# Four-layer stage of a language-model tower: layer norms as eight 64-column operations with two per-partition scalars, in place of two operations of 512 columns

## The reference, cut to what matters

```python
def _layernorm(x, g, b):
    mu = x.mean(-1, keepdims=True)
    var = ((x - mu) ** 2).mean(-1, keepdims=True)
    return (x - mu) * jax.lax.rsqrt(var + EPS) * g + b

for i in range(4):
    h = _layernorm(x, ln1_g[i], ln1_b[i])
    x = x + _linear_attn(h, Wq[i], Wk[i], Wv[i], Wo[i], bo[i])
    h = _layernorm(x, ln2_g[i], ln2_b[i])
    x = x + (gelu(h @ W1[i] + b1[i]) @ W2[i] + b2[i])
```

## Time and profile before

| what | before |
|---|---|
| device time, median of 3 runs (lowest to highest) | 598.67 us (596.02 to 600.78) |
| span of the profiled execution | 593.9 us |
| PE / DVE / ACT busy over the span | 90% / 70% / 64% |
| DVE instructions | 1114 |
| four-layer stage (first second-layer norm to the norm behind the last beat) | 254.2 to 443.5 us of the span |
| mean granted TensorE clock | 0.971 |

### The profile page before, as it was taken

The page is one execution under the profiler, slowest core; times in us unless marked ns, Lnnn a source line. Parts: engine busy times, 40 slices in busy tenths (PEclk is TensorE's granted clock), DMA queues, the critical chain, the costliest instruction groups (busy, mean ns, idle before and its releaser), DMA issues.

```text
span 593.9 us, 8251 instructions
## 1 busy us (share of the span) xinstructions
PE 534.8 (90%) x2798; PEld 279.4 (47%) x2798; DVE 413.9 (70%) x1114; ACT 381.5 (64%) x619; POOL 16.9 (3%) x29
## 2 busy tenths in 40 slices
PE   1898899999999997779999999999847999999995
PEld 1555685334333333656666676666524333333331
DVE  6887797566627555898999999999876336334343
ACT  0379746655666653448888887888734656765653
POOL 4060000000000000000000000000000000000000
PEclk9989998999999998979999999999988999999998
DMA  7910010422131313000000000000000312222220
GB/s 202 252 26 1 6 49 1 128 53 72 37 93 43 95 59 106 1 1 1 1 1 1 1 2 1 1 1 1 1 1 4 108 54 72 76 81 81 69 89 18
DMA packets 26840, 28.08 MB, mean 47 GB/s; under 512 B 12240, under 2 KB 17392, under 8 KB 26736
## 3 DMA queue, kind: packets, MB, share of 16 engines
q1 hardware_dynamic: 24496, 26.98, 16.1%
q10 hardware_dynamic: 2304, 0.58, 0.6%
HBM read 26.24 MB, written 1.31 MB: 46 GB/s over the span
## 4 chain that ended last, share of the span: by engine, by line
PE 51%; DVE 32%; issue 6%; ACT 6%; DMA 3%; SPq 1%; DVEq 0%; ACTq 0%
PE bank L1509 21%; PE bank L1520 20%; DVE l1mom L1240 3%; DVE Xs L1233 3%; DMA Ph<-in_itok 2%; PE bank L1355 2%; DVE Xn L1265 2%; DVE small L1201 2%; DVE Cen L1246 2%; DVE Mm L1226 1%; DVE ksm L1170 1%; DVE Ph L1195 1%; DVE small L1189 1%; ACT Hd L735 1%; PE bank L1422 1%
## 5 line engine op out<-in xcount | busy, mean ns | idle before, releaser
L647 ACT ACTIVATE Hd<-bank,b1all 128x512 f32<-128x512 f32 x256 | 154.9, 688 | 89.0 <-PE bank L1509 88.9
L1520 PE MATMUL bank<-Hd,w2m 128*64 128x512 f32 x512 | 123.7, 605 | 0.9 <-DVE Rest L1084 0.9
L1084 DVE SCALAR_TENSOR_TENSOR Tmp<-bank,b2col,Wb 128x512 f32<-128x512 f32 x56 | 42.0, 750 | 105.7 <-PE bank L1520 104.8
L1520 PEld LDWEIGHTS bank<-Hd,w2m 128*64 128x64 f32 x512 | 31.2, 136 | 85.9 <-issue 80.3
L1509 PE MATMUL bank<-Ph,w1m 64*128 64x512 f32 x256 | 65.2, 628 | 1.3 <-DVE Sc L1015 1.3
L1509 PE MATMUL bank<-XT,w1m 64*128 64x512 f32 x256 | 65.3, 625 | 0.0
L735 ACT ACTIVATE Hd<-bank,lvecs 128x512 f32<-128x512 f32 x64 | 38.7, 688 | 3.3 <-PE bank L1678 3.1
L1509 PEld LDWEIGHTS bank<-XT,w1m 64*128 64x128 f32 x256 | 23.0, 190 | 37.5 <-issue 18.9
L1629 PE MATMUL bank<-bd,XT 128*128 128x128 f32 x256 | 35.9, 285 | 5.2 <-ACT Hd L735 5.1
L1629 PEld LDWEIGHTS bank<-bd,XT 128*128 128x128 f32 x256 | 32.0, 196 | 17.8 <-ACT Hd L735 16.8
L1088 DVE TENSOR_TENSOR Rest<-Rest,Tmp 128x512 f32<-128x512 f32 x56 | 38.7, 692 | 1.9
(11 more groups left out here) (212 smaller groups left out, 825.6 us busy)
## 6 DMA issues: line engine op xcount, KB each, us to landing
Wb<-gate_rows SPq DMA_DIRECT2D x128, 128.0 KB, 2.9
Ph<-in_x SPq DMA_DIRECT2D x4, 512.0 KB, 9.3
Ph<-in_itok SPq DMA_DIRECT2D x4, 384.0 KB, 10.0
w1m<-in_w1e SPq DMA_DIRECT2D x1, 1028.0 KB, 19.2
w2m<-in_w2e SPq DMA_DIRECT2D x2, 512.0 KB, 13.7
w1m<-in_w1e SPq DMA_DIRECT2D x1, 1024.0 KB, 5.5
out<-Hs SPq DMA_DIRECT2D x16, 64.0 KB, 2.1
Hd<-in_w1all SPq DMA_DIRECT2D x1, 512.0 KB, 15.0
```

Of the source, the lines that this page charges most:

```text
L647: ac.activation(Hd[:, st.ring, k // 2, k % 2, :], bank[k][:, :], func, bias=b1all[:, st.m, st.e, k // 2:k // 2 + 1]).then_inc(up_read, 1)
L1084: ve.scalar_tensor_tensor(dst, bank[st.down_bank][:, :], b2, Wb[:, st.t % RING, :], ALU.add, ALU.mult).then_inc(down_read, 1)
L1520: ins = te.matmul(bank[st.down_bank][h * D:(h + 1) * D, :], w2m[:, st.e, hc * D:(hc + 1) * D], Hd[:, st.ring, hc, h, :], start=(hc == 0), ...
```

## The change

The helper centre and its semaphores go. scaled now makes a whole norm from Xs: for each of the eight tiles of a group one tensor_scalar instruction on 64 columns subtracts the tile's mean and multiplies with its inverse root, both read as per-partition scalars (128x1 each). Every one of the eight raises normed by one, so the counts that the matrix engine waits for are multiplied with E = 8; first_norms, which feeds the same semaphore before the beats, raises it by 8 at once.

```diff
-        centred = [sem(f"centred{w}") for w in range(2)]
@@ first_norms
-                                     ALU.mult).then_inc(normed[0], 1)
+                                     ALU.mult).then_inc(normed[0], E)
@@ 
-            def centre(job, w, ring, nth):
-
-                dve.wait_ge(l1_means[w], 4 * nth)
-                ve.tensor_tensor(tiles(Cen, job.g), tiles(Xs, job.g), wide(l1mom[:, ring, w, :, 1], E),
-                                 ALU.subtract).then_inc(centred[w], 1)
@@ 
-            def scaled(job, w, nth):
+            def scaled(job, w, ring):
 
                 rstep.settle()
-                dve.wait_ge(centred[w], nth)
-                ve.tensor_tensor(tiles(Xn, job.g), tiles(Cen, job.g), wide(l1stat[:, 2, w * E:(w + 1) * E], E),
-                                 ALU.mult).then_inc(normed[w], 1)
+                x, y = tiles(Xs, job.g), tiles(Xn, job.g)
+                for e in range(E):
+                    ve.tensor_scalar(y[:, e, :], x[:, e, :], l1mom[:, ring, w, e, 1:2],
+                                     l1stat[:, 2, w * E + e:w * E + e + 1], ALU.subtract,
+                                     ALU.mult).then_inc(normed[w], 1)
@@ beat of VectorE
-                if old:
-                    centre(old, 0, old.ring, old.done)
                 if now:
                     queries_shift(now)
@@ 
                     roots(attn, old)
-                    centre(attn, 1, attn.ring, attn.done)
                 if old:
-                    scaled(old, 0, old.done)
+                    scaled(old, 0, old.ring)
                 if attn:
-                    scaled(attn, 1, attn.done)
+                    scaled(attn, 1, attn.ring)
@@ beat of the matrix engine
-                    pe.wait_ge(normed[0], now.done)
+                    pe.wait_ge(normed[0], E * now.done)
@@ 
-                    pe.wait_ge(normed[1], feed.done)
+                    pe.wait_ge(normed[1], E * feed.done)
```

## The result

The changed kernel takes 615.68 us (median of 4 runs, 613.21 to 619.2) against 597.35 of the kernel before (4 runs, 595.54 to 600.78): a ratio of 1.030, 95% interval 1.025 to 1.035. The forecast was 614.5 us, in a range of 601 to 623. The profiled span grew from 593.9 to 614.2 us.

The account below looks back on a forecast made before the run. DVE's own instruction order was taken to bound beats 3 to 14; +15.0 us from twelve two-norm beats and +0.84 from beats 1 and 16, in all +15.8 on the 598.7 us median, gave 614.5 us, range 601 to 623.

Parts of the forecast that it names:

- DVE's order bounds beats 3 to 14: Four-layer stage: DVE's own instruction order sets the 12.04 us beat, so each us added there moves the end as much.
- The step: Start-to-start time of each new 64-column tensor_scalar with two per-partition scalars: 0.229 us, both scalars paid in full.
- the rival of the free scalars: Rival for the new instruction: scalars cost nothing in a row, step 0.098 us, kernel faster at 592.6 us; chance 0.07.
- the second scalar that comes with the first: Rival for the new instruction: the second scalar adds nothing, step 0.165 us, total 601.3 us; chance 0.12.
- one column at a time: Rival: the short instruction runs at single rate, step 0.263 us, total 621.7 us; 0.11, shared with otherwise dearer steps.
- At no cost: In a beat, the earlier shift, the residual add and their banks, 0.60 us earlier, were to add nothing.
- the prediction's own sign of being wrong: Wrong if the step is below 0.15 us, or a beat grows by other than sixteen steps less 2.41 us.
- the sum: Total added time: +15.0 us from twelve beats with both norms, +0.84 from beats 1 and 16, in all +15.8.
- Beats 2 and 15 hide their norm: One-norm beats ending in DVE waits for ScalarE of 1.48 and 1.47 us, which were to hide the +0.42 us.
- Beats 1 and 16: One-norm beats with the norm on the path: +0.42 us each, 1.83 for 1.41, together +0.84.
- The gain that a cheaper step could bring: In a beat of the stage, at most 0.40 us before DVE waits for ScalarE's exponential.
- The granted clock stays 1.00: The matrix engine was to keep its full clock from 282 us on; losing it, 638 us, had chance 0.04.

Follow-up runs that it names:

- half tiles: The changed kernel with every 64-column operation cut into two of 32 columns and the counts of normed doubled: one run of 666.67 us.
- the kernel with constants: The changed kernel with two constants in place of the two per-partition scalars, mean and inverse root left out of both norms: 597.67 us, 0.998 of the kernel before.

## Why the prediction was right, point by point

- **DVE's order bounds beats 3 to 14, and a loss there is paid in full.** Right: no wait of DVE for another engine in the changed kernel, a beat of 13.38 us for 13.3 foretold.
- **The step.** Right: 0.223 for 0.229 us, 308 ns for "about 0.31". The experiments with no and one scalar give 0.10 and 0.163, where the bounds taken from the earlier trace rows were 0.098 and 0.165. So the rival of the free scalars and that of the second scalar that comes with the first both fall, and the half tiles exclude one column at a time, by which 32 columns less would have taken 33 ns off the step and not 16.
- **At no cost.** Here a step failed. I said that the earlier place of the shift costs nothing and that the wait behind the roots remains as it is. Centre stood between the maximum and the shift and hid the shift's wait; without it the shift starts 0.70 us behind the maximum, where centre had started 0.59 behind it, and the first scaled operation stands 0.08 further behind the roots than centre did. 0.19 us a beat, some 2.3 us in twelve beats, which the sum lacks. By the prediction's own sign of being wrong, a growth other than sixteen steps less 2.41, this part of it is wrong: the beat grew by 1.34 us, the steps by 1.16. The sum took 0.1 us a beat too much for the steps, so that the sum came out at 15.8, where stage and beat 1's norm together (254.23 to 442.22 before, 252.94 to 457.89 after) give 17.0.
- **Beats 2 and 15 hide their norm.** Right: their waits shrank from 1.48 and 1.47 to 1.02 us.
- **Beats 1 and 16.** Beat 1's norm takes 1.79 us for 1.41, and 0.08 more for the doubled wait: +0.46 for +0.42. Beat 16, from beat 15's queries_sum to the norm behind the stage, grew by the same 0.46 (427.12 to 442.22 before, 442.33 to 457.89 after).
- **The gain that a cheaper step could bring.** Mis-sized. I read DVE's distance from ScalarE's exponential in beat 8 as 0.40 us. That beat held the one idle stretch of the earlier trace rows, 0.25 us, and was so much longer than the others; the distance is 12.03 - 11.84 = 0.19 us. The rival's 592.6 us should have read about 595; the kernel with constants took 597.7.
- **The granted clock stays 1.00.** Right in beats 3 to 14, where PE's longest idle stretch is 1.0 us; not behind the stage, where the later return of the clock cost 3.2 and 4.6 us in two profiles. The sum has no term for that part. By medians the change is 18.3 us, of which the runs explain 17.0 in the stage; against 23 later runs of the kernel before (median 598.76) it is 16.9, so the rest is within the spread of the runs.
- **The number.** That 615.68 lies only 1.2 us from 614.5 is in part luck: the medians differ by 2.5 us more than the sum, and the median to which the sum was added was 1.3 us lower with a fourth run.

## What to carry to other kernels

A per-partition scalar is not free: here each adds 0.06 us to an instruction's step, so that splitting one wide operation into eight pays only where the columns saved outweigh eight times the fixed part and the scalars. An operation that is taken out may have been hiding its neighbour's wait: look at what stood right behind it. The distance to the next limit is read from the parts of its loop over several beats, not from one beat, and a second and third limit can lie within 3% of the first.

## What the runs showed of the hardware that I had not expected

- A 16-column tensor_scalar stood still for 0.75 us while GpSimd ran a tensor_tensor (0.92 for 0.17 us), while the tensor_tensor and reduce instructions that ran beside the old job's centre kept their durations (0.67 to 0.69 us). Each of those reads an operand from a bank of PSUM; a tensor_tensor with both operands in SBUF never ran beside a centre. So what GpSimd costs VectorE depended on which VectorE instructions stood beside it.
- The granted clock fell in each beat when PE stood idle for 2.65 us in one stretch (half tiles, mean 0.90 over 17 us), and stayed at 1.00 with 1.0 us (the changed kernel).
- Behind the gap of PE at the end of the stage (5.7 us before, 6.1 after), the clock came back about 4 us after PE had resumed, or more than 12.
